# The first half's maxima in two steps of two pairs, and its exponentials pair by pair behind them

## Chip, core and metric

One core of a Trainium2 chip runs the whole kernel in one launch. The metric is the device time in microseconds (us); lower is better. TensorE is called PE, VectorE DVE, ScalarE ACT, GpSimd POOL and SyncE, which issues all DMAs, SP.

## What is computed

A block of 8 sequences of 512 tokens, 128 features, 16 heads of 8 features: layer norm and modulation, causal attention with rotary position, gated residual; then layer norm, a squared-ReLU network and a spike count, gated residual again. Cut to what matters here:

```python
qkv = h @ qkv_w.T + qkv_b
q, k, v = split(qkv); q = apply_rope(q); k = apply_rope(k)
attn = einsum('bqhd,bkhd->bhqk', q, k) / sqrt(8)
attn = softmax(where(causal, attn, -1e9), axis=-1)
out = einsum('bhqk,bkhd->bqhd', attn, v) @ proj_w.T + proj_b
```

## The kernel before

**Halves, pairs, units.** The 8 batches are cut into 16 halves (n = 0 to 15) of 8 heads, and the heads of a half into 4 pairs. For each half PE computes the scores twice. The first time they lie with queries on partitions (`scores_for_max`, L456), in 21 units of at most 512 columns (`S_BANKS`, NS = 21), and DVE takes the negated maximum of each row (`maxima`, L817, the reduce at L828). There are three banks for that (`s_bank`), so a unit waits until DVE has freed the unit three before it (`reach(pe, s_free, k - 2)`). The second time they lie with keys on partitions (`scores_for_exp`, L491), in 18 slots (`T_BANKS`, NU = 18) in two banks (`t_bank`); ACT takes the exponential of a slot (L703), and PE multiplies the probabilities with v into `o_bank` (`probs_times_v`, L510, L519), in pieces named by key block after the slots in `PV_AFTER` and `PV_LATE`.

**How the maxima get into the second product.** The maximum is subtracted by two more rows of the features (rows `KS` to `KX` of `qf`). When all units of a half are reduced, POOL splits the maxima into two bf16 parts (`split_maxima`, L1075), PE transposes them into `a_bank` (`transpose_maxima`, L478, L488), ACT copies them to `mrow` (`maxima_out`, L705, L709), and SP places them in `qf` with a DMA (`place_maxima`, L361, L364). `scores_for_exp` waits for that DMA at the first slot of a half (L494).

**Order.** Each engine has its order written out by hand. PE's main loop runs over the 288 slots u: the score units up to `scores_ahead(u)`, then the slot, then pieces of other work (`probs_times_v`, and the tasks of the next batch and of the batch before, by `A_AT`, `D_AT`). `scores_ahead` (L88) keeps the score units `S_LEAD` = 31 ahead: 31 units stand before slot 0, and a unit of half 2 (k = 42) first stands ahead of slot 9. Before slot 0 every unit is followed by `keep_warm`, matmuls into `t_bank` whose result is not used.

**Features by way of DRAM.** q and k of a batch are rotated on DVE (`rotary`, L858), summed and split into three bf16 parts by POOL and ACT (`rotary_sum`, `left`, `take_part`), stored to `q_scr` and `k_scr` by SP (`store_part`, L333, L339) and spread from there into `qf` and `kf` (`spread`, L341: one DMA L353 for q, three L359 for k, 1152 KB for a half). Three halves fit (`RING` = 3). PE waits for the spread of half n at its first unit (L461).

**SP's queue in the start.** SP works through one list and waits in place. After the spreads of halves 0 and 1 it issues the ones row, an x load, `g_scr` (the gates, L400), waits until that is stored, issues `rows<-g_scr` (the gates broadcast to 128 partitions, 1536 KB, L402), then the q parts of batch 1, `place_maxima(0)`, the k parts of batch 1 and the spread of half 2:

```python
            for j in range(NPART):
                store_part(1, 0, j)
            place_maxima(0)
            for j in range(NPART - 1):
                store_part(1, 1, j)
```

POOL waits for `rows` at L1174. `place_values` (L716) copies v of a batch out of `a_bank`; for batch 1 PE computes it behind slot 0 (`A_AT[0]`).

Of the kernel before, what the change touches and what calls it, by code (L numbers as in the profile page):

```python
# [12 lines left out]
P = 128  # L13
# [31 lines left out]
S_BANKS += [[(p, 1, 128 * p) for p in range(HP)]]  # L45
S_SECOND = next(k for k, bank in enumerate(S_BANKS) if bank[0][0] >= 2)
# [8 lines left out]
NU = len(T_BANKS)  # L55
PLACE_OF = {(p, kb): (v, col) for v, bank in enumerate(T_BANKS) for p, kb, col in bank}
# [4 lines left out]


# [3 lines left out]
PV_LATE = {0: (3, 5), 1: (4,)}  # L66
PV_USED = [1] * 4 + [3] * 4 + [5] * 4 + [7] * 4 + [8] * 2
# [14 lines left out]
M_AT = 13  # L82

# [4 lines left out]
def scores_ahead(u):  # L88
    return min(NS * HALVES, -(-(u + 1) * NS // NU) + S_LEAD)

# [29 lines left out]
def adaln_kernel(nc, x, wqk, bqk, wv, bv, wo, bo, wfc, wpr, ct, wmod, cosn, sinn, place, out):  # L120
# [9 lines left out]
    with ExitStack() as ctx:  # L130
# [56 lines left out]
        mparts = sb("mparts", [P, NC, MR, HP], BF16)  # L187
        mrow = sb("mrow", [MR * HP, 2 * SEQ], BF16)
# [71 lines left out]
        feat = [sem(f"feat{k}") for k in range(RING)]  # L260
        maxrow = [sem("maxrow0"), sem("maxrow1")]
# [52 lines left out]
        def _(sp):  # L314
# [45 lines left out]

            def place_maxima(n):  # L361
                sp.wait_ge(m_free, n + 1)
                dst = qf[KS:KX, n % RING].rearrange("r (p a) c -> r p (a c)", a=2)
                sp.dma_start(dst, mrow[:, :]).then_inc(maxrow[n % 2], 16)  # L364
# [23 lines left out]
            for qk in range(2):  # L388
                for j in range(NPART):
# [21 lines left out]
            for b in range(NB):  # L411
                if b + 1 < NB:
                    store_part(b + 1, 1, 2)
                    spread(2 * b + 2)
                if b > 0:
                    move_outputs(b - 1, 1)
                    spread_reciprocals(b - 1, 1)
# [25 lines left out]
        def _(pe):  # L443
# [33 lines left out]

            def transpose_maxima(n):  # L478
                pe.wait_ge(mparts_done, n + 1)
                reach(pe, m_free, n)  # L480
# [29 lines left out]
            def probs_times_v(n, kb):  # L510
# [4 lines left out]
                pe.wait_ge(e_done, NU * n + PLACE_OF[HP - 1, kb][0] + 1)  # L515
# [8 lines left out]
            def a_task(b, task):  # L524
                if task == T1:

                    reach(pe, m_free, 2 * (b - 1))
# [4 lines left out]
                elif task < V_:  # L532
                    i = task - QK
                    alone = b == 0 and i == 1
                    if alone:
                        pe.wait_ge(d_free, 1)
                    else:
# [3 lines left out]
                else:  # L541
                    pe.wait_ge(a_free, 3 * b + (2 if b == 0 else 3))
                    reach(pe, m_free, 2 * b - 1)
# [7 lines left out]
            def d_task(b, task, tokens=range(NT)):  # L551
                if task == PROJ:
                    pe.wait_ge(gates_out, 1)
# [11 lines left out]
                elif task < Y_:  # L565
                    i, bank = task - FC, d_bank
                    if b == final - 1:
                        bank = late_hidden[i]
                        pe.wait_ge(s_free, NS * HALVES)
                        pe.wait_ge(m_free, HALVES)  # L570
# [49 lines left out]
            for k in range(NS):  # L620
# [4 lines left out]
            for k in range(NS, NS + 3):  # L625
                scores_for_max(k)
                keep_warm(t_bank[1], 160)
            transpose_maxima(0)
            for k in range(NS + 3, scores_ahead(-1)):
# [4 lines left out]
            for u in range(SLOTS):  # L634
# [5 lines left out]
                for kb in PV_AFTER.get(v, ()):  # L640
# [6 lines left out]
                if at in A_AT and b + 1 < NB:  # L647
# [23 lines left out]
            pe.wait_ge(m_free, HALVES)  # L671
# [25 lines left out]
        def _(act):  # L697
            def exponentials(u):
                n, v = divmod(u, NU)
# [4 lines left out]

# [553 lines left out]
```

## Time and profile before

| | us |
|---|---|
| median of 3 runs | 460.37 (456.43 to 461.63) |
| the profiled execution, its own time | 458.5 |
| span of its trace | 456.8 |
| PE busy in the span | 391.4 (86%) |
| DVE busy | 322.9 (71%) |
| ACT busy | 260.0 (57%) |

The span runs from the first to the last instruction; 1.7 us of the execution's own time lie outside it. Start times below are us from the start of the span. A row of the timeline may merge several instructions (x2 and so on), and what stands in brackets is the idle time ahead of it and what ended it. `PEclk` is the granted TensorE clock as a share of 2.4 GHz.

### The profile page before, as it was taken

The page shows a single profiled execution, that of the slowest core. Times are in us where ns is not written, and L with a number is a line of the kernel's source. Part 1 is how long each engine was busy: PE and PEld are TensorE (multiplying, and loading weights), DVE is VectorE, ACT ScalarE, POOL GpSimd, SP SyncE. Part 2 cuts the span into 40 slices and gives each one's busy share as a digit, 9 for nine tenths or more (in the row PEclk, how much of TensorE's full clock was granted, in tenths as well). Part 3 has the DMA queues.
Part 4 walks back from the last instruction along what each step waited for, and adds up shares of the span by engine and source line. Part 5 has one row for each costly group of instructions (what it writes and reads, how often), then busy time and mean ns, then how long its engine had stood idle before and what let it go on. Part 6 is the DMA issues. An engine that isn't in the chain of part 4 may idle for free.

```text
span 456.8 us, 15637 instructions
## 1 busy us (share of the span) xinstructions
PE 391.4 (86%) x6611; PEld 252.2 (55%) x6611; DVE 322.9 (71%) x722; ACT 260.0 (57%) x449; POOL 124.3 (27%) x159
## 2 busy tenths in 40 slices
PE   3768979878999998899989989999899899878882
PEld 2226755545656665576557655766466657445532
DVE  5669858957883998479965996599839845530745
ACT  7202346576577566665695568666675666477220
POOL 7725002421351143304340325133510400220210
PEclk9899999999999999999999999999999999899998
DMA  6055723242314242323324251415141410110000
GB/s 207 23 171 143 234 75 104 67 123 70 112 57 122 71 108 62 101 80 93 89 83 114 52 136 61 130 28 140 52 126 45 113 46 5 27 30 23 24 1 24
DMA packets 26048, 38.53 MB, mean 84 GB/s; under 512 B 5794, under 2 KB 20714, under 8 KB 23690
## 3 DMA queue, kind: packets, MB, share of 16 engines
q1 hardware_dynamic: 25978, 37.53, 28.7%
q8 instruction: 52, 0.85, 0.8%
q14 instruction: 18, 0.15, 0.1%
HBM read 26.35 MB, written 8.65 MB: 77 GB/s over the span
## 4 chain that ended last, share of the span: by engine, by line
PE 44%; DVE 17%; DMA 13%; ACT 8%; SPq 7%; issue 7%; POOL 2%; POOLq 0%; ACTq 0%; DVEq 0%
PE d_bank L448 10%; PE o_bank L519 9%; PE t_bank L501 6%; PE s_bank L468 6%; DMA den<-o_raw 5%; SPq L370 4%; DVE negmax L828 4%; DMA kf<-k_scr 3%; ACT probs L703 3%; PE a_bank L448 3%; DMA rden<-r_scr 2%; DVE rot_s L864 2%; DVE xn L844 2%; SPq L374 2%; DVE count L895 2%
## 5 line engine op out<-in xcount | busy, mean ns | idle before, releaser
L828 DVE TENSOR_REDUCE negmax<-s_bank 128x1 f32<-128x448 f32 (+7 forms) x368 | 192.0, 564 | 69.0 <-PE s_bank L474 67.5
L703 ACT ACTIVATE probs<-t_bank 128x512 f32<-128x512 f32 x288 | 163.4, 595 | 85.8 <-PE t_bank L506 79.5
L468 PE MATMUL s_bank<-kf,qf 126*64 126x448 bf16 (+7 forms) x1024 | 117.4, 292 | 18.4 <-DVE negmax L828 11.7
L501 PE MATMUL t_bank<-qf,kf 128*64 128x512 bf16 (+7 forms) x1024 | 112.8, 290 | 11.6 <-ACT probs L703 10.9
L468 PEld LDWEIGHTS s_bank<-kf,qf 126*64 126x64 bf16 x1024 | 49.7, 110 | 50.2 <-DVE negmax L828 28.5
L519 PE MATMUL o_bank<-probs,v 128*32 128x512 f32 (+7 forms) x1024 | 76.2, 416 | 0.0
L474 PE MATMUL s_bank<-causal,identb 128*64 128x64 bf16 x1024 | 72.5, 194 | 0.0
L506 PE MATMUL t_bank<-causal_t,identb 128*64 128x64 bf16 x1024 | 64.7, 195 | 0.0
L501 PEld LDWEIGHTS t_bank<-qf,kf 128*64 128x64 bf16 x1024 | 41.4, 111 | 32.0 <-ACT probs L703 14.2
L506 PEld LDWEIGHTS t_bank<-causal_t,identb 128*64 128x64 bf16 x1024 | 48.0, 111 | 9.2
L474 PEld LDWEIGHTS s_bank<-causal,identb 128*64 128x64 bf16 x1024 | 47.4, 111 | 8.4 <-issue 8.1
L519 PEld LDWEIGHTS o_bank<-probs,v 128*32 128x32 f32 x1024 | 26.9, 110 | 37.2 <-issue 25.5
L1078 POOL CAST mparts<-negmax 128x32 bf16<-128x32 f32 x16 | 3.4, 211 | 126.9 <-DVE negmax L828 126.9
L1100 POOL TENSOR_TENSOR whole<-rot_c,rot_s 128x512 f32<-128x512 f32 x15 | 19.1, 1272 | 54.7 <-DVE rot_s L864 54.7
L448 PE MATMUL d_bank<-wpr_sb,sq 128*64 128x128 f32 x512 | 33.7, 276 | 0.0
L448 PEld LDWEIGHTS d_bank<-wpr_sb,sq 128*64 128x64 f32 x512 | 27.5, 137 | 4.7 <-issue 3.5
L753 ACT CAST parts<-whole 128x512 bf16<-128x512 f32 x15 | 9.3, 618 | 35.3 <-POOL whole L1100 35.3
L448 PE MATMUL d_bank<-h2T,wfc_sb 128*64 128x512 f32 x96 | 25.5, 609 | 4.5 <-ACT relu L742 4.5
L1110 POOL TENSOR_TENSOR parts<-rest,parts 128x512 bf16<-128x512 f32 x15 | 17.5, 1169 | 23.0 <-ACT parts L753 23.0
L864 DVE SCALAR_TENSOR_TENSOR rot_s<-a_bank,bqk_sb,sin_sb 64x512 f32<-64x512 f32 x30 | 22.5, 750 | 1.0
L709 ACT COPY mrow<-a_bank 8x1024 bf16<-8x1024 bf16 x16 | 16.0, 1000 | 11.7 <-PE a_bank L488 11.7
L448 PE MATMUL a_bank<-hT,wqk_sb 128*64 128x512 f32 x60 | 16.9, 643 | 4.4 <-DVE rot_s L864 3.1
(115 smaller groups left out, 432.6 us busy)
## 6 DMA issues: line engine op xcount, KB each, us to landing
qf<-q_scr SPq DMA_DIRECT2D x15, 576.0 KB
kf<-k_scr SPq DMA_DIRECT2D x45, 192.0 KB
q_scr<-parts SPq DMA_DIRECT2D x24, 128.0 KB, 1.7
k_scr<-parts SPq DMA_DIRECT2D x24, 128.0 KB, 1.7
xa<-in_x SPq DMA_DIRECT2D x8, 256.0 KB, 4.0
o_t<-o_raw SPq DMA_DIRECT2D x60, 32.0 KB, 2.1
rden<-r_scr SPq DMA_DIRECT2D x15, 128.0 KB
out_y<-count SPq DMA_DIRECT2D x7, 256.0 KB, 7.6
```

Source lines behind the costliest of these rows:

```text
L370: sp.dma_start(den[16 * j:16 * (j + 1), half, :], o_raw[32 * j + 16:32 * j + 32:HD, half, :])\
L448: last = nc.tensor.matmul(bank[own, cols], weights[:, own], data, start=start, stop=stop)
L468: nc.tensor.matmul(bank[C * a:C * (a + 1), col:col + keys], qf[0:KS, slot, 2 * p + a, C * i:C * (i + 1)], kf[0:KS, slot, 2 * p + a, 0:keys ...
L474: last = nc.tensor.matmul(bank[C * a:C * (a + 1), end - C:end], identb[:, C * a:C * (a + 1)], causal[:, C * a:C * (a + 1)], start=False, s ...
L501: nc.tensor.matmul(bank[C * a:C * (a + 1), col:col + w], kf[0:KX, slot, 2 * p + a, C * kb:C * (kb + 1)], qf[0:KX, slot, 2 * p + a, C * kb: ...
L506: last = nc.tensor.matmul(bank[C * a:C * (a + 1), col:col + C], identb[:, C * a:C * (a + 1)], causal_t[:, C * a:C * (a + 1)], start=False, ...
L519: last = nc.tensor.matmul(o_bank[32 * p:32 * (p + 1), C * kb:SEQ], v32[:, b % 2, NP * kb + HP * half + p, :], probs[:, v, col:col + w], st ...
L703: nc.scalar.activation(probs[:, v, :], t_bank[u % 2][:, :], ACT.Exp, scale=SCALE).then_inc(e_done, 1)
L828: last = nc.vector.tensor_reduce(own[:, i, p:p + len(same)], cols, AX.X, ALU.max, negate=True)
L864: nc.vector.scalar_tensor_tensor(dst[to, qk, :], bank[of, :], bqk_sb[of, qk:qk + 1], table[of, :], ALU.add, ALU.mult).then_inc(rotated if ...
L1100: nc.gpsimd.tensor_tensor(whole[:, qk, :], rot_c[:, qk, :], rot_s[:, qk, :], ALU.add)\
L1110: nc.gpsimd.tensor_tensor(parts[:, qk, 2, :], rest[:, qk, :], parts[:, qk, 1, :], ALU.subtract).then_inc(split_done, 1)
```

## The change

Half 0 is treated apart. Its maxima are split, transposed, copied and placed in two steps: pairs 0 and 1 first (`pairs` = 0), pairs 2 and 3 after (`pairs` = 1). The unit that holds key block 1 of all pairs moves from the end of each half's units to the place behind the first two pairs' units (position 10), so that 11 units complete the first step. Half 0's slots go in `FIRST_ORDER`: nine slots of pairs 0 and 1, then nine of pairs 2 and 3, and its products with v go behind slots 14 and 16 and not 9 and 13. 22 units stand before slot 0 and each slot adds 2 until the former lead is reached. The q/k and v tasks of batch 1 move ahead on PE (k into `d_bank` before unit 0, v behind unit 5), `place_values(1)` on ACT with them. On SP the `rows<-g_scr` broadcast moves behind the spread of half 2, and POOL's wait for it behind `split_maxima(1)`.

```diff
+NS_FIRST = len(S_BANKS) // 2 + 1
+S_BANKS.insert(NS_FIRST - 1, [(p, 1, 128 * p) for p in range(HP)])
+S_SECOND = NS_FIRST - 1
...
+FIRST_ORDER = sorted(range(NU), key=lambda v: T_BANKS[v][0][0] >= 2)
+S_START = 22
+S_RISE = 2
+PV_AFTER_FIRST = {14: (0, 1, 7), 16: (2, 6)}
+M_SECOND = 4
...
-    return min(NS * HALVES, -(-(u + 1) * NS // NU) + S_LEAD)
+    return min(NS * HALVES, -(-(u + 1) * NS // NU) + S_LEAD, S_START + S_RISE * (u + 1))
...
+            def place_first_maxima(pairs):
+                sp.wait_ge(m_free, pairs + 1)
+                dst = qf[KS:KX, 0, HP * pairs:HP * (pairs + 1)].rearrange("r (p a) c -> r p (a c)", a=2)
+                sp.dma_start(dst, mrow[0:MR * 2, :]).then_inc(first_rows[pairs], 16)
...
-            sp.wait_ge(gates_stored, 16)
-            sp.dma_start(rows[:, :, :, :].rearrange("p w b f -> p (w b f)"),
-                         g_scr.rearrange("r f -> (r f)").unsqueeze(0).to_broadcast([P, 3 * NB * P]))\
-                .then_inc(rows_loaded, 16)
...
-            place_maxima(0)
-            for j in range(NPART - 1):
+            place_first_maxima(0)
+            for j in range(NPART):
                 store_part(1, 1, j)
+            place_first_maxima(1)
...
+                if b == 0:
+                    sp.wait_ge(gates_stored, 16)
+                    sp.dma_start(rows[:, :, :, :].rearrange("p w b f -> p (w b f)"),
...
+            def transpose_first_maxima(pairs):
+                pe.wait_ge(mparts_done, pairs + 1)
+                reach(pe, m_free, pairs)
...
             def scores_for_exp(u):
-                n, v = divmod(u, NU)
-                if v == 0:
-                    pe.wait_ge(maxrow[n % 2], 16 * (n // 2 + 1))
+                n, at, v = bank_at(u)
+                if n == 0 and at in (0, N_FIRST):
+                    pe.wait_ge(first_rows[at // N_FIRST], 16)
...
+            a_task(1, QK + 1)
+            for k in range(NS_FIRST + 4):
                 scores_for_max(k)
                 keep_warm(t_bank[1], 160)
-                if k == 6:
-                    a_task(1, QK + 1)
...
+                if k == 5:
+                    a_task(1, V_)
+            transpose_first_maxima(0)
...
+                if u == M_SECOND:
+                    transpose_first_maxima(1)
...
-            maxima_out(0)
+            take_part(1, 0, 0)
+            place_values(1)
+            take_part(1, 0, 1)
+            first_maxima_out(0)
...
+                if u == M_SECOND + 1:
+                    first_maxima_out(1)
...
-            for k in range(7):
+            for k in range(NS_FIRST):
                 maxima(k)
             for step in range(3):
-                rotary(1, 1, step)
+                rotary(1, 1, step, bank=d_bank)
...
-            split_maxima(0)
-            pool.wait_ge(rows_loaded, 16)
+                split_first_maxima(qk)
 
             for b in range(NB):
                 split_maxima(2 * b + 1)
+                pool.wait_ge(rows_loaded, 16)
```

SP's DMAs from the ones row on, in the kernel before (`mrow` holds the maxima, `q_scr` and `k_scr` are the parts' DRAM tensors):

```order
L396 DMA kf<-ones_row 2x24x512
L331 DMA xa<-in_x 128x4x128
L400 DMA g_scr<-gate_t 24x128
L402 DMA rows<-g_scr 128x3072
L339 DMA q_scr<-parts 128x512 x3
L364 DMA qf<-mrow 2x4x1024
L339 DMA k_scr<-parts 128x512 x3
L353 DMA qf<-q_scr 72x1x4096
L359 DMA kf<-k_scr 24x1x4096 x3
```

The same stretch in the changed kernel:

```order
L437 DMA kf<-ones_row 2x24x512
L367 DMA xa<-in_x 128x4x128
L441 DMA g_scr<-gate_t 24x128
L375 DMA q_scr<-parts 128x512 x3
L400 DMA qf<-mrow 2x2x1024
L375 DMA k_scr<-parts 128x512 x3
L400 DMA qf<-mrow 2x2x1024
L389 DMA qf<-q_scr 72x1x4096
L395 DMA kf<-k_scr 24x1x4096 x3
L456 DMA rows<-g_scr 128x3072
```

The single placing of the maxima has become two, one ahead of the k parts of batch 1 and one between them and the spread of half 2; the broadcast now stands behind that spread.

ACT from the copy of the gates to the first exponentials (`probs`), in the kernel before:

```order
L774 COPY gate_t<-d_bank 24x128
L753 CAST parts<-whole 128x512
L753 CAST parts<-rest 128x512
L753 CAST parts<-whole 128x512
L753 CAST parts<-rest 128x512
L709 COPY mrow<-a_bank 8x1024
```

In the changed kernel:

```order
L845 COPY gate_t<-d_bank 24x128
L824 CAST parts<-whole 128x512
L795 COPY v<-a_bank 64x64x8 x2
L824 CAST parts<-rest 128x512
L772 COPY mrow<-a_bank 4x1024
L824 CAST parts<-whole 128x512
L824 CAST parts<-rest 128x512
L766 ACTIVATE probs<-t_bank 128x512 x5
L772 COPY mrow<-a_bank 4x1024
L766 ACTIVATE probs<-t_bank 128x512 x9
```

The first copy of maxima stands ahead of the casts of k, the second behind five exponentials, and the copy of v ahead of the second cast of q.

## Rows read from the trace of the kernel before

**Rows 1.** Windows: busy us of each engine, PEclk, DMA share, GB/s.
```profile
30.50:52.60 22.10, 19.58 (x329) 14.37 (x329) 21.12 (x40) 3.73 (x6) 7.62 (x8) 1.00 0.66 192
52.60:72.20 19.60, 15.46 (x342) 10.78 (x340) 13.72 (x33) 12.32 (x21) 3.35 (x6) 1.00 0.31 84
...
142.20:191.00 48.80, 44.98 (x804) 29.47 (x804) 37.93 (x85) 31.60 (x56) 14.67 (x18) 1.00 0.33 90
```
**Rows 2.** Timeline of PE: start, duration, instruction, idle before and releaser.
```profile
29.45 1.08 PE L448 MATMUL a_bank<-hT,wqk_sb 128*64 128x512 f32 x4 [0.29 <-ACT hT L713]
...
47.88 0.61 PE L488 MATMUL a_bank<-identb,mparts 128*8 128x128 bf16 x8
...
52.64 0.38 PE L501 MATMUL t_bank<-qf,kf 128*64 128x512 bf16 x2
...
52.89 1.13 PE L546 MATMUL a_bank<-wv_sb,hT 128*64 128x64 f32 x32
...
62.44 0.41 PE L468 MATMUL s_bank<-kf,qf 126*64 126x512 bf16 x2 [2.90 <-DMA kf<-k_scr]
...
70.37 0.41 PE L501 MATMUL t_bank<-qf,kf 128*64 128x256 bf16 x4 [0.28 <-ACT probs L703]
...
72.17 0.41 PE L501 MATMUL t_bank<-qf,kf 128*64 128x512 bf16 x2 [0.19 <-DMA qf<-mrow]
```
**Rows 3.** Timeline of SP, in the start.
```profile
49.56 0.66 SPq L364 DMA_DIRECT2D qf<-mrow  x1
50.26 2.13 SPq L339 DMA_DIRECT2D k_scr<-parts  x3
52.49 0.84 SPq L353 DMA_DIRECT2D qf<-q_scr  x1
53.84 2.08 SPq L359 DMA_DIRECT2D kf<-k_scr  x3
```
**Rows 4.** Chain of waits in order of time: start, us, what.
```profile
55.27 7.12 DMA kf<-k_scr
```
**Rows 5.** Timelines of SP and PE, spread of half 4 and its first unit.
```profile
95.49 0.85 SPq L353 DMA_DIRECT2D qf<-q_scr  x1
...
105.33 0.41 PE L468 MATMUL s_bank<-kf,qf 126*64 126x512 bf16 x2 [1.13 <-DMA kf<-k_scr]
```
**Rows 6.** Timelines of DVE and ACT in the start.
```profile
31.37 1.53 DVE L864 SCALAR_TENSOR_TENSOR rot_s<-a_bank,bqk_sb,sin_sb 64x512 f32<-64x512 f32 x2
32.93 3.67 DVE L828 TENSOR_REDUCE negmax<-s_bank 128x1 f32<-128x512 f32 x7
...
36.90 0.75 DVE L864 SCALAR_TENSOR_TENSOR rot_c<-a_bank,bqk_sb,cos_sb 128x512 f32<-128x512 f32 x1 [0.30 <-PE a_bank L448]
...
39.25 9.32 DVE L828 TENSOR_REDUCE negmax<-s_bank 128x1 f32<-128x320 f32 x19
...
48.53 1.00 ACT L709 COPY mrow<-a_bank 8x1024 bf16<-8x1024 bf16 x1 [5.32 <-PE a_bank L488]
53.10 0.60 ACT L703 ACTIVATE probs<-t_bank 128x512 f32<-128x512 f32 x1 [3.57 <-PE t_bank L506]
```
**Rows 7.** Windows (columns of rows 1) around three idle stretches of PE.
```profile
60.00:62.00 2.00, 0.00 (x0) 0.00 (x0) 0.08 (x1) 0.17 (x1) 0.46 (x2) 1.00 0.50 142
...
388.00:392.00 4.00, 2.31 (x70) 1.89 (x67) 3.10 (x8) 2.08 (x4) 0.00 (x0) 0.98 0.13 29
392.00:396.00 4.00, 4.00 (x43) 1.58 (x40) 3.82 (x7) 1.13 (x2) 0.46 (x2) 0.60 0.17 48
...
450.00:456.00 6.00, 0.00 (x0) 0.00 (x0) 4.19 (x11) 0.00 (x0) 0.00 (x0) 0.77 0.14 44
```
**Rows 8.** DMA issues from 43.9 to 46 us, and of the whole span: KB each, us to landing.
```profile
rows<-g_scr SPq DMA_DIRECT2D x1, 1536.0 KB, 6.7
q_scr<-parts SPq DMA_DIRECT2D x3, 128.0 KB, 6.6
...
q_scr<-parts SPq DMA_DIRECT2D x24, 128.0 KB, 1.7
```

More of the change, by code:

```diff
@@ L55 @@
 NU = len(T_BANKS)
+FIRST_ORDER = sorted(range(NU), key=lambda v: T_BANKS[v][0][0] >= 2)
+N_FIRST = sum(bank[0][0] < 2 for bank in T_BANKS)
 PLACE_OF = {(p, kb): (v, col) for v, bank in enumerate(T_BANKS) for p, kb, col in bank}
@@ L187, in adaln_kernel @@
         mparts = sb("mparts", [P, NC, MR, HP], BF16)
+        mparts_flat = mparts[:, :, :, :].rearrange("p i r h -> p i (r h)")
+        mparts_first = [mparts_flat[:, :, 2 * MR * k:2 * MR * (k + 1)].rearrange("p i (r h) -> p i r h", r=MR)
+                        for k in range(2)]
         mrow = sb("mrow", [MR * HP, 2 * SEQ], BF16)
@@ L476, in scores_for_max @@
                 last.then_inc(s_ready, 1)
+            def transpose_first_maxima(pairs):
+                pe.wait_ge(mparts_done, pairs + 1)
+                reach(pe, m_free, pairs)
+                pe.wait_ge(v_placed, 2 * 2)
+                for i in range(NC):
+                    to = m_bank[0:MR * 2, :].rearrange("m (a q) -> m a q", a=2)[:, :, C * i:C * (i + 1)]
+                    last = nc.tensor.transpose(to, mparts_first[pairs][:, i].rearrange("p r h -> p (r h)"), identb[:, :])
+                last.then_inc(m_ready, 1)
             def transpose_maxima(n):
-                pe.wait_ge(mparts_done, n + 1)
-                reach(pe, m_free, n)
+                pe.wait_ge(mparts_done, rows_made(n))
+                pe.wait_ge(m_free, rows_made(n - 1))
                 if n % 2 == 0:
@@ L533, in a_task @@
                     i = task - QK
-                    alone = b == 0 and i == 1
-                    if alone:
+                    alone = b < 2 and i == 1
+                    if alone and b == 0:
                         pe.wait_ge(d_free, 1)
+                    elif alone:
+                        pe.wait_ge(gates_out, 1)
+                        pe.wait_ge(a_free, 3 + QK)
                     else:
@@ L619, in _ @@
             gates_out_of_columns()
[L620 removed]
+            a_task(1, QK + 1)
+            for k in range(NS_FIRST + 4):
                 scores_for_max(k)
                 keep_warm(t_bank[1], 160)
[L623 to L629 removed]
+                if k == 5:
+                    a_task(1, V_)
+            transpose_first_maxima(0)
+            for k in range(NS_FIRST + 4, scores_ahead(-1)):
                 scores_for_max(k)
@@ L639, in _ @@
                 scores_for_exp(u)
-                for kb in PV_AFTER.get(v, ()):
+                for kb in (PV_AFTER if n else PV_AFTER_FIRST).get(v, ()):
                     probs_times_v(n, kb)
@@ L703, in exponentials, with first_maxima_out @@
                 nc.scalar.activation(probs[:, v, :], t_bank[u % 2][:, :], ACT.Exp, scale=SCALE).then_inc(e_done, 1)
-            def maxima_out(n):
-                act.wait_ge(m_ready, n + 1)
-                if n > 0:
-                    act.wait_ge(maxrow[(n - 1) % 2], 16 * ((n - 1) // 2 + 1))
+            def first_maxima_out(pairs):
+                act.wait_ge(m_ready, pairs + 1)
+                if pairs:
+                    act.wait_ge(first_rows[0], 16)
+                nc.scalar.copy(mrow[0:MR * 2, :], m_bank[0:MR * 2, :]).then_inc(m_free, 1)
+            def maxima_out(n):
+                act.wait_ge(m_ready, rows_made(n))
+                if n == 1:
+                    act.wait_ge(first_rows[1], 16)
+                else:
+                    act.wait_ge(maxrow[(n - 1) % 2], rows_placed(n - 1))
                 nc.scalar.copy(mrow[:, :], m_bank[0:MR * HP, :]).then_inc(m_free, 1)
@@ L774, in _ @@
             nc.scalar.copy(gate_t[:, :], d_bank[0:3 * NB, 0:P]).then_inc(gates_out, 1)
-            for j in range(2):
-                take_part(1, 0, j)
+            take_part(1, 0, 0)
+            place_values(1)
+            take_part(1, 0, 1)
+            first_maxima_out(0)
             for j in range(2):
                 take_part(1, 1, j)
-            maxima_out(0)
             TAKE_AT = {-9: (0, 0), -7: (0, 1), -5: (1, 0), -3: (1, 1)}
@@ L793, in _ @@
                     outputs(n - 1)
-                if at == 1 and b + 1 < NB:
+                if at == 1 and 0 < b < final:
                     place_values(b + 1)
@@ L818, in maxima @@
                 n, unit = divmod(k, NS)
-                if unit == 0:
-                    reach(dve, mparts_done, n - 1)
+                if unit == 0 and n > 1:
+                    dve.wait_ge(mparts_done, rows_made(n - 2))
                 dve.wait_ge(s_ready, k + 1)
@@ L983, in _ @@
                 rotary(1, 0, step)
-            for k in range(7):
+            for k in range(NS_FIRST):
                 maxima(k)
             for step in range(3):
-                rotary(1, 1, step)
-            for k in range(7, scores_ahead(-1)):
+                rotary(1, 1, step, bank=d_bank)
+            for k in range(NS_FIRST, scores_ahead(-1)):
                 maxima(k)
```

53 lines of the change are left out of this document (38 added, 15 removed).

## Prediction

> **What bounds the kernel now.** I read the windows by stage first. In a full batch PE is busy 44.98 of 48.80 us at full clock and DVE 37.93: PE sets the pace there, and this row stands for four full batches in a row of 48.2 to 48.8 us [rows 1], so whatever the start gains or loses is carried to the end. The two stages that the change touches are different. From 30.5 to 52.6 us DVE is busy 21.12 of 22.10: the score units wait for the reduces, PE fills its gaps with warm matmuls, and ACT does almost nothing (3.73) because no exponential may start. From 52.6 to 72.2 PE is busy only 15.46 of 19.60, so 4.1 us are idle.
>
> PE's timeline then says where. The transposes of the maxima run at 47.88, the first slot at 52.64, and one idle stretch stands out: 2.90 us before 62.44, ended by the DMA that spreads k of half 2 [rows 2]. The first slot of half 1 waits 0.19 for the placed maxima at 72.17, and one slot 0.28 for ACT at 70.37. So the start has two gates in a row: the maxima (first slot at 52.64) and the features of half 2 (unit 42 at 62.44). SP's timeline shows what holds the second: SP waits in its list for the copy of the maxima, places them at 49.56, stores the k parts at 50.26, issues the q spread at 52.49 and the k spread from 53.84 [rows 3]. In the chain of waits the last k DMA stands from 55.27 for 7.12 us, to 62.39 [rows 4]. Hence from the q issue to the landing 9.9 us; half 4 confirms it, 95.49 to 105.33 = 9.84 [rows 5].
>
> **The first gate, step by step.** Up to the end of the rotary step of q at 32.90 nothing on DVE changes. The first step of the maxima needs 11 units. Before, 7 took 3.67 us and the next 17 units (19 reduces) 9.32, that is 0.55 each [rows 6]; so 3.67 + 4 x 0.55 = 5.9. Two PE tasks now stand among the units: the k matmuls ahead of unit 0 (1.08) and those of v behind unit 5 (1.13) [rows 2]. The first ends about when DVE is ready, but takes PE's lead away; with both DVE waits some 1.2 us by my count. The 11th unit is reduced near 32.9 + 5.9 + 1.2 = 40.0. The rotary of k follows on DVE, 0.75 + 1.53 [rows 6], to 42.3. The turning of the first two pairs hides behind this: POOL's split, PE's transposes (behind unit 14, which needs the 12th reduced, so 43.5), the copy of 1.00 (to about 45.3), the DMA of some 2.3. It would land near 47.7. Then slot 0 stands behind unit 23, which needs 21 reduced: 10 more units, 5.5 us, to 47.8. Slot 0 comes at about 48.3 in place of 52.64: this gate opens 4.3 us earlier. The smaller edits (8 more transposes of 0.61 in all, a second ACT copy of 1.00, two small POOL operations, the earlier place of v) cost nothing more, because they end in front of the stall that comes next; with that cover gone they would cost up to 1.6 on PE and ACT.
>
> **The second gate.** Here lies what decides. In SP's new list the spread of half 2 stands behind the second placing, and that waits for ACT's second copy, which stands behind five exponentials. So count to it: slot 4 stands behind unit 31, which needs 29 reduced, 8 more than slot 0: 8 x 0.55 = 4.4, slot 4 at 52.5. From slot to exponential 0.46 (52.64 to 53.10), the exponential 0.60, the copy 1.00 [rows 2, 6], SP's placing 0.66 [rows 3]: the q spread is issued at 55.3. Before it was 52.49: 2.8 us later. The k parts no longer hold it (they are stored by about 51), so the k DMAs follow at once. Their landing: by the time from the q issue 9.9 us, so 65.2; by the time from the last k issue (0.84 + 1.4 behind the q issue, then 7.1), 64.6; and as an outer bound, if the quiet queues help, 7.1 from the q issue, 62.4. I take 65.1, +2.7 against 62.44, because both spreads measured sit at 9.8 to 9.9.
>
> By then PE has done what it had done before at this point plus one slot (unit 42 now stands ahead of slot 10, not 9), 0.3 us of work. It reaches unit 42 at about 58.5, since 11 more units from slot 4 on take 6 us of DVE, and stands idle 6.6 us in place of 2.9. The products with v are behind slots 14 and 16, so none of them fills the gap; they come later, but they came behind the gap before too, so their sum of work doesn't change. What it does change: the maxima of half 1 are turned sooner after the gap, and the 0.19 + 0.28 of waits at 70.37 and 72.17 should go [rows 2]. Sum so far: +2.7 - 0.3 - 0.5 = +1.9.
>
> **The clock.** The trace grants full clock through the 2.90 us gap (PEclk 1.00 in 60 to 62), but falls to 0.60 in 392 to 396 after a stretch in which PE was busy 2.31 of 4 us, and to 0.77 in 450 to 456 where PE has nothing to do [rows 7]. A gap of 6.6 us is well past the one that was forgiven, so I expect half clock (1.2 GHz) behind it. In the row of 392 to 396 a mean of 0.60 over 4 us is 3.2 us at half rate; PE loses half of that, 1.6. Some of it may lie in the gap itself. I take 1.5; bounds 0 (as with the shorter gap) and 1.6.
>
> The Trainium skill, "TensorE: Matmul & The Clock Gate", section "HAM oscillation — how this bites in real kernels", says that an array kept waiting for a transfer comes back at half clock and pays for it in the next piece of work. By that rule the sum is +3.4; by the row of the 2.90 us gap alone it would stay +1.9. The fall at 392 in this trace agrees with the rule, the gap at 60 doesn't.
>
> **The broadcast.** `rows` (1536 KB) moves from ahead of the q parts to behind the spread of half 2, issued near 58. Its old place cost: q stores issued just behind it took 6.6 us to land where 1.7 is usual [rows 8]. The same row says that a transfer issued behind another lands behind it, so the broadcast should not hold up the spread, only what follows: landing by about 71, before the placing of half 1's maxima (issued near 71) and about when POOL wants it. Cost 0; bound from the other side below.
>
> **Sum.** 458.5 + 1.9 + 1.5 = 461.9 us, against the profiled execution's own 458.5. The median shown, 460.37, is 1.9 above that execution, and the three runs spread over 5.2 us, so this sum may look like +1.5 against the median. A measurement of this kernel can tell about 1% (4.6 us) from no change; +3.4 is inside.
>
> **Rivals.**
> - The quiet queue helps: the spread lands at 62.4, 7.1 us after its q issue. PE's gap is then 3.9 us; +0.0 - 0.3 - 0.5 = -0.8, time 457.7, or with half a clock fall 458.5. For it: k stores ran just ahead of both measured spreads. Against: 9.84 and 9.9 agree although the k issues stood differently. For more than 1% faster it would have to land before 58.6, 3.3 us after its issue.
> - The clock stays up: 460.4. For it: the 2.90 us gap. Against: more than twice as long.
> - The broadcast gets among the spread. At 58 some two thirds of the spread, 0.8 MB, are outstanding; if both share the engines, the spread is held up for as long as 0.8 MB of the broadcast take, at its 1.5 MB in 6.7 us 3.5 us. Then 461.9 + 3.5 = 465.4, slower by 1.5%. It decides from 1.2 us of delay on. Against: the q stores of rows 8, which were not served early. For: the DMA share was 0.50 in the window 60 to 62 [rows 7], so some engines had nothing left of the spread and would take up the broadcast early.
> - The change doesn't do what it says: the first slots aren't earlier (the placing of the first pairs or unit 23 comes at 52 or later). Everything behind moves too, the q spread to 59: 458.5 + 6.5 + 1.5 - 0.8 = 465.7. Nothing in the rows speaks for it.
>
> **How the numbers follow.** Forecast 0.57 (own range 459.5 to 463.5), quiet queue 0.18, clock up 0.10, broadcast 0.12, no earlier start 0.03. The range 457.0 to 466.0 takes in the rivals; the fastest bound (a spread at the broadcast's rate, 5.2 us after its issue, -2.7 in all) and odd sums are left out. Slower by over 1% (beyond 463.1): the last two rivals, 0.15, and 0.08 of the forecast's upper part: 0.23. Faster by over 1%: 0.05, for a loss in the steady batches that I don't see and the change might take away. Within 1%: 0.72.
>
> **What would show each step.** Right: first slot near 48.3; second copy of the maxima ending near 54.6; q spread issued near 55.3; an idle stretch of PE of 6 to 7 us, ended by `kf<-k_scr`, to 65; PEclk near 0.5 behind it; stages beyond 100 us as long as before. Wrong: a first slot later than 50, a gap before unit 42 under 4 us or none, or full clock behind it. A spread that takes over 11 us points to the broadcast. If later batches became shorter or longer than 48.3 us, the argument that the start alone counts is wrong.

## The result, and the profile after the change

The changed kernel takes 464.35 us, median of 4 runs (462.30 to 465.79); the kernel before, run beside it, 458.98 (456.43 to 461.63, 4 runs). The ratio is 1.0097 with a 95% interval of 1.0049 to 1.0145: slower beyond the interval, by a little under 1%. The profiled execution took 463.16 us (span 461.3, mean granted clock 0.980), against 458.5 (456.8, 0.989) before: +4.7, where +3.4 was forecast. The medians differ by 5.4. The ratios here and below leave out executions that took over 1.5% longer than their kernel's fastest, among them two of run 1 (630.71 and 1279.08 us) and one of run 11 (552.07).

First the page's clock row and the windows of the changed kernel (columns of [rows 1]):

```profile
PEclk9898979999999999999999999999999999999998
```
```profile
30.50:52.60 22.10, 19.50 (x313) 13.94 (x311) 19.77 (x36) 6.25 (x11) 8.02 (x10) 0.92 0.44 125
52.60:72.20 19.60, 11.28 (x214) 7.81 (x215) 11.12 (x24) 7.21 (x13) 0.46 (x2) 0.83 0.56 155
...
62.00:64.00 2.00, 0.00 (x0) 0.00 (x0) 0.00 (x0) 0.00 (x0) 0.00 (x0) 1.00 1.08 260
64.00:66.00 2.00, 0.00 (x0) 0.00 (x0) 0.00 (x0) 0.00 (x0) 0.00 (x0) 0.55 1.03 227
66.00:68.00 2.00, 0.17 (x2) 0.17 (x4) 0.00 (x0) 0.00 (x0) 0.00 (x0) 0.50 0.90 299
68.00:70.00 2.00, 2.00 (x18) 0.96 (x18) 1.34 (x3) 0.48 (x1) 0.00 (x0) 0.50 0.71 268
70.00:72.00 2.00, 2.00 (x38) 1.39 (x35) 1.67 (x4) 1.19 (x3) 0.00 (x0) 0.74 0.28 90
...
148.40:197.20 48.80, 44.78 (x808) 29.36 (x804) 38.16 (x85) 31.53 (x57) 14.65 (x18) 1.00 0.33 90
```

The first row is what the change was made for: ACT does 6.25 us of work before 52.6, where it did 3.73 [rows 1]. The second takes more back than that: PE is busy 11.28 us of 19.60 where it was 15.46. From 62 to 66 no engine computes at all while the DMA engines are full, and behind it the clock is at 0.50, that is 1.2 GHz. The full batch in the last row (moved by 6.2 us, so that it covers the same work) is the one of [rows 1] to within 0.3 us of busy time on every engine: nothing has changed there.

PE's timeline of the changed kernel, at the places of [rows 2]:

```profile
42.70 0.38 PE L512 MATMUL s_bank<-kf,qf 126*64 126x448 bf16 x2 [1.82 <-DVE negmax L902]
...
49.70 0.38 PE L557 MATMUL t_bank<-qf,kf 128*64 128x512 bf16 x2
...
54.25 0.61 PE L529 MATMUL a_bank<-identb,mparts 128*4 128x128 bf16 x8
...
67.83 0.64 PE L512 MATMUL s_bank<-kf,qf 126*64 126x512 bf16 x2 [8.04 <-DMA kf<-k_scr]
...
71.90 0.61 PE L542 MATMUL a_bank<-identb,mparts 128*8 128x128 bf16 x8
```

SP's timeline of the changed kernel, to be read against [rows 3]:

```profile
45.10 0.66 SPq L400 DMA_DIRECT2D qf<-mrow  x1
45.80 3.31 SPq L375 DMA_DIRECT2D k_scr<-parts  x3
55.93 0.62 SPq L400 DMA_DIRECT2D qf<-mrow  x1
56.65 0.84 SPq L389 DMA_DIRECT2D qf<-q_scr  x1
57.54 2.08 SPq L395 DMA_DIRECT2D kf<-k_scr  x3
59.66 0.44 SPq L456 DMA_DIRECT2D rows<-g_scr  x1
```

The first slot is at 49.70, 2.9 us earlier than 52.64. SP has issued the stores of the k parts by 49.1 and then does nothing until 55.93, because its next entry, the second placing, waits for ACT's second copy (54.90 to 55.90). The q spread comes 4.2 us later than in [rows 3], and PE's idle stretch before unit 42 has grown from 2.90 to 8.04 us. The first outputs of half 0 leave ACT at 82.05 instead of 75.95, +6.1. The shift stays between 6.1 and 7.2 up to half 13, and ends at +4.5, because the profiled execution of the kernel before loses its clock once more near 392 [rows 7] and this one does not.

The earlier slots do not bring PE to unit 42 sooner in this execution: it arrives at 59.8 (67.83 less 8.04), and before at 59.5 (62.44 less 2.90). DVE's reduces are what it waits for on the way (its timeline in the changed kernel, the stretch up to unit 41):

```profile
47.34 13.26 DVE L902 TENSOR_REDUCE negmax<-s_bank 128x1 f32<-128x320 f32 x27 [0.39 <-PE s_bank L518]
```

They run back to back to 60.6. In this execution the whole stretch is 1.6 us late, because the clock fell at 44 (the section on the prediction has the windows). In the traces of runs 5, 9 and 11, where it did not fall there, the same order of PE reaches unit 42 at 58.2, 1.3 us sooner than the kernel before.

### The profile page after: what moved, and what is told of

It is laid out like the page before. It is cut to its first block, busy times and chain, and to the rows that moved or that the text cites. A ratio compares the mean times of both kernels' runs of the same rounds, so it can differ in the third digit from the quotient of the medians.

```text
span 461.3 us, 15589 instructions
## 1 busy us (share of the span) xinstructions
PE 390.8 (85%) x6583; PEld 251.2 (54%) x6583; DVE 323.4 (70%) x722; ACT 260.8 (57%) x450; POOL 124.7 (27%) x161
## 4 chain that ended last, share of the span: by engine, by line
PE 39%; DVE 16%; DMA 13%; issue 9%; ACT 9%; SPq 8%; POOL 5%; POOLq 0%; ACTq 0%; DVEq 0%
PE d_bank L492 8%; PE o_bank L575 8%; PE t_bank L557 6%; PE s_bank L512 6%; DMA kf<-k_scr 5%; DVE negmax L902 5%; SPq L411 4%; DMA rden<-r_scr 3%; ACT probs L766 3%; DVE xn L918 3%; DMA den<-o_raw 3%; SPq L415 2%; PE a_bank L492 2%; DMA r_scr<-rden_c 2%; POOL rs L1170 2%
## 5 line engine op out<-in xcount | busy, mean ns | idle before, releaser
L902 DVE TENSOR_REDUCE negmax<-s_bank 128x1 f32<-128x512 f32 (+7 forms) x368 | 192.7, 564 | 76.0 <-PE s_bank L518 74.4
L512 PE MATMUL s_bank<-kf,qf 126*64 126x512 bf16 (+7 forms) x1024 | 119.9, 296 | 27.2 <-DVE negmax L902 15.2
L575 PE MATMUL o_bank<-probs,v 128*32 128x512 f32 (+7 forms) x1024 | 75.2, 412 | 0.0
L938 DVE SCALAR_TENSOR_TENSOR rot_s<-a_bank,bqk_sb,sin_sb 64x512 f32<-64x512 f32 x28 | 21.0, 750 | 0.9
L795 ACT COPY v<-a_bank 64x512 f32<-64x512 f32 x16 | 9.3, 580 | 20.5 <-PE o_bank L575 18.8
L1189 POOL TENSOR_TENSOR rest<-whole,parts 128x512 f32<-128x512 f32 x15 | 17.4, 1158 | 10.4 <-ACT parts L824 10.4
```

The costliest lines, as they stand in the source:

```text
L512: nc.tensor.matmul(bank[C * a:C * (a + 1), col:col + keys], qf[0:KS, slot, 2 * p + a, C * i:C * (i + 1)], kf[0:KS, slot, 2 * p + a, 0:keys ...
L575: last = nc.tensor.matmul(o_bank[32 * p:32 * (p + 1), C * kb:SEQ], v32[:, b % 2, NP * kb + HP * half + p, :], probs[:, v, col:col + w], st ...
L902: last = nc.vector.tensor_reduce(own[:, i, p:p + len(same)], cols, AX.X, ALU.max, negate=True)
L938: nc.vector.scalar_tensor_tensor(dst[to, qk, :], bank[of, :], bqk_sb[of, qk:qk + 1], table[of, :], ALU.add, ALU.mult).then_inc(rotated if ...
```

## The experiments

Ratios are to the kernel before, run on the same chip between the others. Medians of the kernel before were 459.7, 460.1, 460.2 and 460.3 us in the four groups (31, 35, 17 and 11 runs).

**1. The spread ahead of the second placing**

```diff
+            spread(2)
             place_first_maxima(1)
...
-                if b + 1 < NB:
+                if 0 < b < final:
                     spread(2 * b + 2)
```

> The changed kernel with SP's spread of half 2 ahead of the second placing of maxima. Theory (the spread's place in SP's list decides, and the start carries over to the end): q spread issued near 49.2 us in place of 56.65, landed near 59.5; PE's gap before unit 42 shrinks from 8.04 us to under 1.5, no half clock behind it; time 8 to 9 us below the changed kernel's, about 455.5, some 3 us under the kernel before. Rival A (the turn in two steps itself costs, or later stages absorb the start): the gap goes, but the time stays within 3 us of the changed kernel's 464. Rival B (the small placing DMA, now behind 1152 KB of spread, comes late): slot 9 waits for it, up to 4 us in place of the gap, time near 459.

0.9929 [0.9891, 0.9968]: faster than the kernel before, and 1.7% below the changed kernel's ratio. SP's and PE's timelines of this kernel (the profiled execution took 461.93 us where the median of ten is 457.53; only the order and distances in the start are read from it):

```profile
50.34 0.95 SPq L389 DMA_DIRECT2D qf<-q_scr  x1
...
55.53 0.67 SPq L400 DMA_DIRECT2D qf<-mrow  x1
...
62.95 0.41 PE L558 MATMUL t_bank<-qf,kf 128*64 128x512 bf16 x2 [3.79 <-DMA qf<-mrow]
```

Unit 42, which stands behind slot 9, finds its features there and waits for nothing. The order of SP's list is thus the cause of the loss. But the gap has partly moved, as rival B has it: the 8 KB of maxima, issued behind the spread, take 7.4 us to land, slot 9 waits 3.79 for them, and the clock still falls behind that wait (0.50 in 64 to 66).

**2. The second turn earlier**

```diff
-M_SECOND = 4
+M_SECOND = 1
```

> The changed kernel with the second transpose behind slot 1 and not 4, so ACT's second copy stands behind two exponentials. Theory: copy near 52.9, q spread issued near 53.7 (3.0 us earlier), unit 42 near 64.9, time 3 us below the changed kernel's, near 461. Rival (the spread's landing isn't tied to its issue, but to the broadcast or the k parts): the issue moves 3 us, unit 42 less than 1.5 us.

1.0033 [0.9995, 1.0072], median 462.00. SP and PE:

```profile
52.60 0.62 SPq L400 DMA_DIRECT2D qf<-mrow  x1
53.33 0.84 SPq L389 DMA_DIRECT2D qf<-q_scr  x1
...
64.44 0.64 PE L512 MATMUL s_bank<-kf,qf 126*64 126x512 bf16 x2 [4.90 <-DMA kf<-k_scr]
```

The q spread comes 3.32 us earlier and unit 42 3.39: one for one, as the argument of the second gate has it. (The two traces can be set side by side because both lost about as much to the clock ahead of this: here the first placing is issued at 46.40, 1.3 us late, and the changed kernel lost 1.6 behind its first placing.) The median is 2.4 us below the changed kernel's, but the intervals of the two ratios overlap.

**3 and 4. Warm matmuls into the gap** (6 of them, then 8, ahead of unit 42)

```diff
+                if u == 10:
+                    pe.wait_ge(e_done, 9)
+                    keep_warm(t_bank[0], SEQ, 8)
```

> The changed kernel with six warm matmul pairs of 512 columns (6.5 us at full clock, result not used) in PE's gap before unit 42. Theory of the clock: no half clock from 64.4 to 71.2, unit 42 at 67.8 as before, the units and slots behind it at their full rate; 1.5 to 1.7 us below the changed kernel's time. Rival: the clock stays up, but PE then waits for DVE, so under 0.5 us is gained; or the warm matmuls slow something else and nothing is gained.

> The changed kernel with eight warm pairs in the gap and not six (six left 3.62 us idle behind them, and the clock still fell to half from 68.3 on). Theory of the clock: 8.6 us of warm work, unit 42 at 68 to 69, PEclk 1.00 behind it, the stretch from unit 42 to the transposes of half 1's maxima 2.8 to 3.0 us in place of 4.07; time 1.5 us below the changed kernel's. Rival: DVE bounds that stretch anyway, which then shortens by less than 0.5 us.

With 6, 1.0064 [1.0031, 1.0096]: 3.62 us of the gap were left over, the clock still fell (0.50 from 68 on), so its trace says nothing of what the clock costs. With 8, 1.0045 [1.0017, 1.0072]. PE's timeline and one window of the kernel with 8:

```profile
67.35 0.41 PE L512 MATMUL s_bank<-kf,qf 126*64 126x512 bf16 x2 [1.02 <-DMA kf<-k_scr]
...
70.37 0.61 PE L542 MATMUL a_bank<-identb,mparts 128*8 128x128 bf16 x8
```
```profile
68.00:70.00 2.00, 1.81 (x41) 1.12 (x35) 2.00 (x4) 1.15 (x3) 0.00 (x0) 1.00 0.61 237
```

The clock is full, and PE does 41 matmuls in the window in which the changed kernel did 18. From unit 42 to the transposes of half 1 it takes 3.02 us instead of 4.07: the clock costs 1.05 us there, and nothing behind it, since in the changed kernel it is back at full before the transposes (1.00 from 71.2 on). The medians do not show this: that of 8 warm pairs is 1.9 us below the changed kernel's, with intervals that overlap, but that of 6, where the clock fell, is as low (462.18 against 462.42).

**5. The broadcast into the idle queue, ahead of the second placing**

```diff
+            sp.wait_ge(gates_stored, 16)
+            sp.dma_start(rows[:, :, :, :].rearrange("p w b f -> p (w b f)"),
...
             place_first_maxima(1)
```

> The changed kernel with the broadcast of the gates issued in the quiet time behind the k parts (near 49.2 us) and not behind the spread of half 2. Theory (the broadcast got among the spread): landing 9.9 us after the q issue in place of 11.2, unit 42 at 66.5, 1.3 us below the changed kernel's time. Rival (the spread takes 11.2 us for another reason): unit 42 stays at 67.8, same time.

1.0078 [1.0035, 1.012]. SP and PE:

```profile
55.05 0.84 SPq L389 DMA_DIRECT2D qf<-q_scr  x1
...
65.27 0.64 PE L511 MATMUL s_bank<-kf,qf 126*64 126x512 bf16 x2 [7.07 <-DMA kf<-k_scr]
```

From the q issue to unit 42 it takes 10.2 us, not 11.2. The median, 464.99, is not better for it.

**6. ACT's queue issues the second placing, SP goes on**

```diff
+                if pairs:
+                    act.wait_ge(m_free, pairs + 1)
+                    dst = qf[KS:KX, 0, HP * pairs:HP * (pairs + 1)].rearrange("r (p a) c -> r p (a c)", a=2)
+                    act.dma_start(dst, mrow[0:MR * 2, :]).then_inc(first_rows[pairs], 16)
```

> The changed kernel; the second placing of maxima is issued by ACT on its own queue right behind its copy, so SP goes on from the k parts to the spread of half 2. Theory (SP's place in the list cost 8 us; in the run with the spread first, slot 9 waited 3.79 us only because the placing stood behind the spread in one queue): q spread near 50, unit 42 no later than 61, slot 9 waits under 1 us, gap under 2 us, no half clock behind it; 2 us below the run with the spread first, near 455. Rival (the placing shares the 16 DMA engines with the spread whatever queue it is on): slot 9 still waits 3 to 4 us, same time as the run with the spread first, near 457.5.

0.9987 [0.9951, 1.0022]. The timeline of ACT's queue and of PE:

```profile
57.16 1.26 ACTq L775 DMA_DIRECT2D qf<-mrow  x1
...
64.12 0.41 PE L556 MATMUL t_bank<-qf,kf 128*64 128x512 bf16 x2 [3.23 <-DMA qf<-mrow]
```

A queue of its own did not help the small DMA: it lands 7.0 us after its issue, about as late as behind the spread on SP, though here spread and broadcast were both ahead of it. It also costs ACT 1.26 us. The spread itself did what the theory says, issued at 50.33 and there for unit 42; the rival holds for slot 9, and the median (460.66) is above what either forecast. In this execution the clock was at 0.67 from 44.0 to 47.3, and slot 0 came at 50.93, which pushes the placing back too.

**7. The same in the kernel before** (ACT places the maxima of half 0)

```diff
-            place_maxima(0)
...
+                if n == 0:
+                    act.wait_ge(m_free, 1)
+                    dst = qf[KS:KX, 0].rearrange("r (p a) c -> r p (a c)", a=2)
+                    act.dma_start(dst, mrow[:, :]).then_inc(maxrow[0], 16)
```

> The kernel before; only the placing of half 0's maxima goes to ACT's queue, so that SP goes on to the k parts and the spread of half 2. Theory (the stall before unit 42 is a matter of SP's list alone, and the two-step turn isn't needed to remove it): k parts stored near 48, q spread near 48.5, unit 42 near 59.5 with a gap under 0.5 us in place of 2.90, time 2.5 to 3 us below the kernel before, near 456.5. Rival (the broadcast, still in its old place from 43.8 us, delays the placing on ACT's queue too): slot 0 comes later than 52.64 by up to 2 us and half of the gain goes.

0.9991 [0.9958, 1.0024]. My theory fell: the q spread is still issued at 52.74, although SP was free of the placing. SP's timeline of this kernel:

```profile
44.29 0.34 SPq L402 DMA_DIRECT2D rows<-g_scr  x1
44.67 1.67 SPq L339 DMA_DIRECT2D q_scr<-parts  x3
46.39 1.86 SPq L339 DMA_DIRECT2D k_scr<-parts  x3
52.74 0.82 SPq L353 DMA_DIRECT2D qf<-q_scr  x1
```

SP sits idle from 48.3 to 52.7. What it waits for, 4.4 us by the list of SP's waits, are the stores of the q parts, which take 6.8 us to land behind the broadcast. Unit 42 came at 63.08, after a gap of 2.21 us. In the kernel before, the spread is held twice: by the placing in SP's list and, as long, by 1.5 MB that stand in the queue ahead of its inputs.

**8. The kernel before, only the broadcast moved behind the spread**

```diff
-            sp.wait_ge(gates_stored, 16)
-            sp.dma_start(rows[:, :, :, :].rearrange("p w b f -> p (w b f)"),
...
                     spread(2 * b + 2)
+                if b == 0:
+                    sp.wait_ge(gates_stored, 16)
+                    sp.dma_start(rows[:, :, :, :].rearrange("p w b f -> p (w b f)"),
```

> The kernel before with only the broadcast of the gates (and POOL's wait for it) moved as the change moves it, behind the spread of half 2. Theory (issued behind, it still slows the spread by about 1 us): q spread issued at 52.4 as before, unit 42 1.0 to 1.3 us later than 62.44, time 1 us above the kernel before. Rival (the k parts, no longer behind the broadcast, land sooner and make up for it): unit 42 within 0.5 us of 62.44.

1.004 [1.0008, 1.0072]. SP and PE, and a window:

```profile
51.84 0.84 SPq L353 DMA_DIRECT2D qf<-q_scr  x1
...
63.70 0.64 PE L469 MATMUL s_bank<-kf,qf 126*64 126x512 bf16 x2 [4.06 <-DMA kf<-k_scr]
```
```profile
62.00:64.00 2.00, 0.30 (x2) 0.18 (x4) 0.00 (x0) 0.00 (x0) 0.00 (x0) 0.50 0.90 323
```

The spread is issued 0.65 us earlier than in [rows 3] and lands 11.9 us after its issue instead of 9.9; the gap is 4.06 and the clock falls. Set against run 10, the same kernel with no broadcast in the start, where the spread took 10.6, the broadcast behind it costs 1.3 us. One pair of traces is thin for that; the section on the prediction has all of them.

**9. The changed kernel, only the broadcast late** (behind the first spread of reciprocals; POOL's first `residual_in` and `gate_projection` with it)

```diff
-                if b == 0:
-                    sp.wait_ge(gates_stored, 16)
...
                 spread_reciprocals(b, 0)
+                if b == 0:
+                    sp.wait_ge(gates_stored, 16)
...
-                residual_in(b)
-                gate_projection(b)
+                if b > 0:
+                    residual_in(b)
+                    gate_projection(b)
...
+                if b == 0:
+                    pool.wait_ge(rows_loaded, 16)
+                    residual_in(0)
+                    gate_projection(0)
```

> The changed kernel with only the broadcast taken out of the start (issued behind the first reciprocals, near 90 us). Theory (the broadcast costs the spread a good 1 us): q spread near 56.5 as before, landing 9.9 to 10.2 us after it, unit 42 near 66.5; time 1.0 to 1.5 us below the changed kernel's. Rival: landing after 11.2 us again, no gain; or the late broadcast holds up the moves of half 0's outputs and the time rises.

1.0119 [1.0063, 1.0174], 464.19 us. SP and PE:

```profile
55.05 0.84 SPq L389 DMA_DIRECT2D qf<-q_scr  x1
...
64.57 0.64 PE L512 MATMUL s_bank<-kf,qf 126*64 126x512 bf16 x2 [6.37 <-DMA kf<-k_scr]
...
75.43 0.81 SPq L389 DMA_DIRECT2D qf<-q_scr  x1
...
86.69 0.64 PE L512 MATMUL s_bank<-kf,qf 126*64 126x512 bf16 x2 [1.88 <-DMA kf<-k_scr]
```

The spread is 9.5 us under way, 1.7 less than with the broadcast behind it. But nothing is gained in time: PE waits 1.88 us for the spread of half 3 and the clock falls in two more stretches (from 86 and from 120). That spread was issued at 75.43 and the broadcast only at 90.72, so its 11.3 us are not the broadcast's doing. Why the kernel is no faster than the changed one (464.35) stays open.

**10. The kernel before, only the broadcast late** (the edit of 9 on the other kernel)

> The kernel before with only the broadcast of the gates taken out of the start (behind the first reciprocals), SP's order of placing and k parts as before. Theory (two things held the spread of half 2 to the same moment, the broadcast ahead of the stores and SP's wait for the copy of the maxima; taking one away gives little, both together gave 2.9 us): q spread at 51.8, landing 9.5 us after it, unit 42 near 61.3 with a gap near 1.8 us, time 1 us below the kernel before. Rival (the broadcast alone was what the last run's gain came from, at the start or in the batches behind): unit 42 within 0.5 us of 59.5, or a time 4 us or more below the kernel before.

0.9891 [0.9856, 0.9926], 455.89 us, median of 6. The gate of unit 42 does not explain it. SP and PE:

```profile
52.92 0.84 SPq L353 DMA_DIRECT2D qf<-q_scr  x1
...
63.53 0.41 PE L469 MATMUL s_bank<-kf,qf 126*64 126x512 bf16 x2 [2.82 <-DMA kf<-k_scr]
```

The gap is as long as before. In this execution the start is 1.2 us late (clock 0.62 in 30 to 32; slot 0 at 53.82 and not 52.64). With that taken off, the q spread is issued at the 51.8 of the theory, but lands 10.6 us later and not 9.5, so unit 42 stays where it was. The profiled execution (460.48) is this kernel's slowest, so its trace does not show where the median's 4 us come from. That stays open.

**11 and 12. Everything in time: the two steps, and the one step**

The SP list is q spread, placing, k spreads; the broadcast is late as in 9 and 10. In the changed kernel, with `M_SECOND = 1`:

```diff
-            place_first_maxima(1)
+            spread(2, between=lambda: place_first_maxima(1))
```

In the kernel before, with the maxima in one step:

```diff
-            place_maxima(0)
-            for j in range(NPART - 1):
+            for j in range(NPART):
                 store_part(1, 1, j)
+            spread(2, between=lambda: place_maxima(0))
```

`between` is called after the q spread's issue and ahead of the k spreads'.

> The changed kernel with three moves at once: the second transpose behind slot 1; on SP the spread of half 2 ahead of the second placing for q and behind it for k; the broadcast of the gates out of the start, behind the first reciprocals (near 85 us), with POOL's two operations that need it behind the k parts of batch 2. Theory (spread, placing and broadcast compete for SP's list and for the same DMA engines): q spread near 50.3, second placing near 53, k spreads by 55.5, unit 42 at 60.3 to 61, slot 9 waits under 1 us, no half clock; 2 us below the run with the spread first, near 455. Rival (the placing lands late behind q's 576 KB alone): slot 9 waits 2 us or more and the time stays near 457.

> The kernel before (one step, its order of slots) with the same two moves on SP: k parts, then the q spread of half 2, the placing of half 0, the k spreads, and the broadcast of the gates behind the first reciprocals. Theory (the start is bound by SP's list and the broadcast, not by the turn in one step): q spread near 46.5, unit 42 near 59.5 with a gap under 0.5 us, slot 0 within 1 us of 52.64; time 3 to 3.5 us below the kernel before, near 456.5, and the two-step version with the same moves is not more than 2 us faster. Rival (two steps are worth their 3 us of earlier slots once the features are there in time): the two-step version is 3 us or more faster than this one.

Two steps: 0.9916 [0.9883, 0.9950], 455.35 us. One step: 0.9884 [0.9840, 0.9928], 453.07 us (6 runs, 451.51 to 454.56), the fastest median of all. SP and PE of the two-step version:

```profile
49.14 0.88 SPq L389 DMA_DIRECT2D qf<-q_scr  x1
51.23 0.65 SPq L402 DMA_DIRECT2D qf<-mrow  x1
51.92 2.09 SPq L397 DMA_DIRECT2D kf<-k_scr  x3
...
60.82 0.41 PE L514 MATMUL s_bank<-kf,qf 126*64 126x512 bf16 x2 [2.67 <-DMA kf<-k_scr]
```

SP's timeline and two windows of the one-step version:

```profile
45.59 0.83 SPq L353 DMA_DIRECT2D qf<-q_scr  x1
49.55 0.69 SPq L366 DMA_DIRECT2D qf<-mrow  x1
50.28 2.05 SPq L361 DMA_DIRECT2D kf<-k_scr  x3
```
```profile
56.00:60.00 4.00, 4.00 (x109) 3.01 (x110) 3.25 (x7) 3.70 (x7) 0.00 (x0) 1.00 0.13 32
52.60:72.20 19.60, 18.39 (x385) 11.99 (x381) 15.93 (x40) 13.45 (x23) 1.68 (x4) 1.00 0.23 68
```

Slot 0 of the one-step version stands at 52.64 as before, and that of the two-step version at 48.10. Even so the one-step version is not the slower one (the intervals overlap): its q spread can go at 45.59, PE has no wait at unit 42, and it is busy 18.39 us of the 19.60 where it was 15.46. The 4.5 us of earlier slots are worth nothing that these two runs show. They do not settle it, though, since the two-step version still waits 2.67 us at unit 42 and the one-step version doesn't.

How much of the gain is the spread's? Against run 9, which has the late broadcast alone, the two-step version is 8.8 us faster. But run 10, the kernel before with the late broadcast alone, has a ratio as low as run 12's (0.9891 and 0.9884). The traces show 3.1 us of run 12's gain in the start (first outputs of half 0 at 72.83 instead of 75.95); the shift grows to 7.0 by the last half, and no run shows what the rest comes from.

## Why the prediction came out as it did

**Right: the two gates and their sign.** The first gate opens earlier, the second is held by SP's list, PE's idle stretch grows and the clock falls behind it, and the batches are unchanged. Run 1 shows it from the one side, run 2 from the other. The forecast was +3.4 us and the profiled executions differ by 4.7. The median of 464.35 lies above the forecast's own range of 459.5 to 463.5 and within the wide one of 457.0 to 466.0, nearer to the rival of the broadcast (465.4) than to the forecast (461.9). The profiled execution's 463.16, for which the sum was worked out, lies inside the first.

**The first gate.** The forecast was slot 0 at 48.3 and the q spread at 55.3. Runs 5 and 9, with the same code up to there, have them at 48.10 and 55.05. In the profiled execution of the changed kernel they are at 49.70 and 56.65, since it spent the stretch behind the 1.82 us gap at 42.7 at half clock, which those two did not. The window of that stretch in the changed kernel, then in run 9:

```profile
44.00:47.30 3.30, 3.30 (x31) 2.46 (x32) 1.91 (x4) 1.90 (x3) 1.16 (x1) 0.52 0.13 46
```
```profile
44.00:47.30 3.30, 3.30 (x68) 2.90 (x68) 3.21 (x8) 1.98 (x3) 1.16 (x1) 1.00 0.20 68
```

PE does 31 matmuls in place of 68, DVE starves, and slot 0 is 1.6 us late. The prediction priced one fall of the clock, behind the long gap, and not one here. It is chance in part: of nine profiled executions with that gap two lost the clock behind it.

**The second gate: the term that failed is "Cost 0" for the broadcast.** I argued from the q stores of [rows 8] that what is issued behind does not slow what is ahead. From the q issue to unit 42 the spread took 11.2 us in the changed kernel, 11.1, 12.0 and 11.1 in runs 2, 3 and 4, and 11.9 in run 8, all with the broadcast right behind it. With the broadcast ahead or away it took 9.9 (before), 10.2 (run 5), 10.3 (run 7), 9.5 (run 9) and 10.6 (run 10). The five are all above the other five, by 1.3 us in the mean, where the rival had 3.5 and said that it decides from 1.2 on. That rival's mechanism was real, only smaller. Its own sign was in my text: the DMA share of 0.50 in 60 to 62. A single trace would not show it: later spreads, with no broadcast near, took from 9.2 to 11.7 us (101.79 to 112.83 in the changed kernel, 358.00 to 369.67 in run 10). For the same reason the 9.84 of [rows 5] confirmed less than I thought.

**The wait at unit 42.** 8.04 us where 6.6 were forecast. PE reached unit 42 at 59.8 and not 58.5, later by 1.3; the landing came 2.7 later than 65.1, of which 1.35 is the late issue and 1.3 the slower spread. The late issue and the late arrival both go back to the clock's fall at 44: in the traces without it the issue is at 55.05 and PE is there at 58.2.

**The clock.** Forecast 1.5, bounds 0 and 1.6. Run 4 measures 1.05 us, with the clock below full up to 71.2. From unit 42 to the first outputs it takes 13.2 us in run 4, 14.2 in the changed kernel, 14.8 in run 5 and 15.0 in run 9, so by these traces a fall behind this gap costs 1.0 to 1.8 us. The rival "clock stays up" did not hold. That PE came back at half rate and paid in the next piece of work is what the Trainium skill, "TensorE: Matmul & The Clock Gate", section "HAM oscillation — how this bites in real kernels", says of an array that waits for a transfer. The trace agrees, with 18 matmuls against 41 in the window from 68 to 70.

**The sum.** Unit 42 is 5.4 us late (67.83 against 62.44), where +2.7 was forecast. From there to the first outputs it takes 14.2 us where it was 13.5, +0.7, just what the terms -0.3, -0.5 and +1.5 add up to; but the clock was 1.05 of it, so the other two made some 0.3 and not 0.8, and two wrong sizes cancel. The first outputs are thus +6.1 late, and the start alone was off by 2.7 us. It ends at +4.5 only since the profiled execution of the kernel before had its own fall at 392. That the forecast came within 1.3 us of the profiled executions' difference is luck to that extent.

**The rivals.** "The quiet queue helps" fell: with no broadcast near, the spread still took 9.5 us. "No earlier start" fell.

**What the prediction did not see** is how little the first gate was worth. Between slot 0, behind unit 23, and unit 42 DVE has 19 more units to reduce, at 0.55 each some 10 us. DVE's timeline in run 9:

```profile
41.95 17.05 DVE L902 TENSOR_REDUCE negmax<-s_bank 128x1 f32<-128x512 f32 x34
```

It reduces without a break from 41.95 to 59.00, so slots that start 4.5 us sooner (48.10 against 52.64) bring PE to unit 42 only 1.3 us sooner (58.2 against 59.5). The prediction had that 58.5, counted one slot of lead, 0.3 us, as gained, and did not say that without the second gate no more than this was to be won.

## What to carry to other kernels

Before a gate is opened earlier, find what sets the pace from there to the next gate: if it is another engine's work, most of the earlier start is idle time moved (here 3.2 of 4.5 us). An in-order DMA queue should not hold a transfer that is needed next behind an entry that waits for compute; first count what is ready, then what is waited for. A bulk transfer right behind an urgent one is not free. Taking it out of the stretch is worth a try and must be measured: the same move gave 4 us on one kernel (run 10) and nothing on the other (run 9).

## What the runs showed of the hardware that I had not expected

- A DMA issued later slows one that is already under way: five spreads with 1536 KB right behind took 11.1 to 12.0 us, five without 9.5 to 10.6, 1.3 us apart in the mean.
- The same spread of 1152 KB took from 9.2 to 11.7 us with no broadcast near, across the batches of these traces.
- 8 KB issued among a spread of 1152 KB take 7.4 us on the same queue and 7.0 us on another engine's queue (there with the broadcast ahead too): a second queue did not bring it sooner.
- Equal gaps do not have equal consequences for the clock. The gap of 1.82 us near 42.7 was followed by half clock in two of nine profiled executions that have it (the changed kernel and run 6, not in runs 1 to 5, 9 and 11); the gap of 1.55 us near 391 cost the clock before, and one of 1.56 us, at 397.63 in the changed kernel, did not.
- One program's executions lie further apart than most effects here: those of the kernel before run from 455.65 to 466.16 us in one group of 35. A difference of 2 us is to be read from many runs, and the trace tells where it arises.
